# Second attention: stacked operands of chunks 1 to 3 by DMA through DRAM, chunk 0 by matmuls; full rows beside the smallest diagonal steps

## What is computed

```
b, s, _ = x.shape                      # 1, 2048; 16 heads of size D = 8, 4 kv heads
q = (x @ Wqa @ Wqb).reshape(b, s, H, D)
kv = (x @ Wkva @ Wkvb).reshape(b, s, KVH, D, 2)
k, v = (kv[..., 0], kv[..., 1])
q, k = _rope(q), _rope(k)              # rotation of pairs of features by position
k, v = repeat(k, 4), repeat(v, 4)      # each kv head serves 4 query heads
out = softmax(causal(q k^T * D ** -0.5)) v   # then @ Wout + bout, times a gate, plus x
```

## Time and profile before

| | us |
|---|---|
| median of 3 runs | 1277.96 |
| range of the runs | 1269.67 to 1278.08 |
| profiled execution, its time | 1279.31 |
| its span, first to last instruction | 1277.5 |
| from the first stack to step 0 | 454.6 to 505.9 |
| the 160 steps | 505.9 to 974 |

### The profile page before, as it was taken

One profiled execution on the slowest core, in us unless ns is written; L12 is line 12 of the kernel. 1 busy time (PEld: TensorE's weight loads), 2 busy tenths in 40 slices (PEclk: granted clock), 3 DMA queues, 4 the chain that ended last, 5 costly groups with the idle time before them and its releaser, 6 DMA issues.

```text
span 1277.5 us, 17760 instructions
## 1 busy us (share of the span) xinstructions
PE 1161.5 (91%) x6079; PEld 624.4 (49%) x6079; DVE 927.9 (73%) x1803; ACT 761.2 (60%) x1120; POOL 174.8 (14%) x142
## 2 busy tenths in 40 slices
PE   3888668999999788999999999999997799999998
PEld 2333344577777423333233222322223688888886
DVE  5699986355555746688896879898933788888885
ACT  1635436588788322456555756566776666666664
POOL 0000010498899400000000000000000000000000
PEclk9898777799999865899997989998999799999999
DMA  5000010789985300000000000000000211111001
GB/s 166 1 0 1 0 46 11 168 195 208 201 190 130 132 1 1 2 2 2 2 1 2 2 1 2 1 2 1 1 2 1 93 58 58 58 57 57 1 1 33
DMA packets 35660, 60.36 MB, mean 47 GB/s; under 512 B 14138, under 2 KB 27706, under 8 KB 30266
## 3 DMA queue, kind: packets, MB, share of 16 engines
q1 hardware_dynamic: 35586, 59.36, 18.4%
HBM read 57.59 MB, written 1.64 MB: 46 GB/s over the span
## 4 chain that ended last, share of the span: by engine, by line
PE 65%; DVE 24%; ACT 5%; issue 4%; POOL 1%; DMA 0%; SPq 0%; DVEq 0%; POOLq 0%; ACTq 0%
PE ps L868 10%; PE ps L1075 10%; PE ps L869 10%; PE ps L870 10%; PE ps L1004 7%; DVE arena_b L1824 6%; PE ps L1053 5%; PE ps L965 4%; DVE arena_b L1575 3%; PE ps L1017 2%; PE ps L1060 2%; DVE arena_b L1756 1%; PE ps L730 1%; POOL parts L685 1%; ACT arena_b L1388 1%
## 5 line engine op out<-in xcount | busy, mean ns | idle before, releaser
L1388 ACT ACTIVATE arena_b<-ps 128x1024 f32<-128x1024 f32 (+3 forms) x320 | 274.9, 895 | 155.0 <-PE ps L1053 133.6
L868 PE MATMUL ps<-parts 128*128 128x512 f32 x640 | 253.6, 396 | 8.7 <-POOL parts L685 6.3
L870 PE MATMUL ps<-parts 128*128 128x512 f32 x640 | 250.3, 391 | 0.0
L869 PE MATMUL ps<-parts 128*128 128x512 f32 x640 | 250.2, 391 | 0.0
L1824 DVE TENSOR_REDUCE arena_b<-ps 128x1 f32<-128x512 f32 x384 | 237.6, 682 | 16.6 <-PE ps L1004 15.2
L1004 PE MATMUL ps<-arena_a 48*128 48x128 bf16 (+3 forms) x832 | 187.2, 323 | 11.1 <-DVE arena_b L1824 3.2
L685 POOL TENSOR_TENSOR parts<-arena_b,parts 128x512 fp32r<-128x512 f32 x128 | 166.8, 1311 | 69.7 <-ACT parts L1325 65.1
L1075 PE MATMUL ps<-arena_b 128*32 128x512 f32 (+3 forms) x1280 | 160.0, 573 | 0.0
L1053 PE MATMUL ps<-arena_a 50*128 50x512 bf16 (+3 forms) x832 | 151.5, 318 | 4.9 <-issue 2.6
L1004 PEld LDWEIGHTS ps<-arena_a 48*128 48x128 bf16 x832 | 60.5, 97 | 185.6 <-DVE arena_b L1824 115.8
L1756 DVE SCALAR_TENSOR_TENSOR arena_b<-ps,arena_a 128x512 f32<-128x512 f32 x128 | 87.0, 688 | 87.5 <-PE ps L870 87.5
(11 more groups left out here) (268 smaller groups left out, 1198.4 us busy)
## 6 DMA issues: line engine op xcount, KB each, us to landing
arena_a<-root_weights SPq DMA_DIRECT2D x60, 512.0 KB, 6.4
arena_b<-expert_weights SPq DMA_DIRECT2D x7, 1024.0 KB, 5.6
wslot<-in_L_ffn_up_w SPq DMA_DIRECT2D x8, 256.0 KB, 6.7
wslot<-in_L_ffn_down_w SPq DMA_DIRECT2D x8, 256.0 KB, 7.3
wslot<-in_L_ffn_w_gate SPq DMA_DIRECT2D x8, 256.0 KB, 2.9
wslot<-in_L_ffn_w_up SPq DMA_DIRECT2D x8, 256.0 KB, 3.3
wslot<-in_L_ffn_w_down SPq DMA_DIRECT2D x8, 256.0 KB, 4.4
arena_b<-in_spread SPq DMA_DIRECT2D x1, 1152.0 KB, 6.2
```

Of the source, the lines that this page charges most:

```text
L868: mm(bank, w(0), x(0), start=start, stop=False)
L869: mm(bank, w(0), x(1), start=False, stop=False)
L870: return mm(bank, w(1), x(0), start=False, stop=stop)
L1388: a(probs[:, s % 2, 2 * pair:2 * pair + 2, off:CW], ps[:, 2 + 2 * pair:4 + 2 * pair, off:CW], ACT.Exp, scale=scale).then_inc(p2_exp, 1)
```

## The change

Only chunk 0 is still stacked by matmuls (12 stacks: 3 ahead, 9 as slots). For chunks 1 to 3 SP writes the split parts `q3` and `k3` to DRAM and loads them back to their strips, once for each product and strip. `kst` gets a second copy: `kst[.., half, ..]` holds keys only in the strip `half`, zeros elsewhere, so that a matmul over all 128 rows gives the same sum as one over the strip; POOL zeroes `kst` and chunks 1 to 3 of `qst` first. `WIDE` says which score slots use 128 rows: those ahead of and beside step 0, and those beside the step that follows a step with 256 or 128 columns left, so the last step of an item and the first of the next. `kst` copies of chunk 0 are two ScalarE instructions. SLOTS[0] now ends with item 0's maxima (16 scores, 3 stacks, 1 maxima), steps 0 and 1 have 8 slots each, and of the 576 scores 139 are wide. POOL's bias addition waits for the fourth item's maxima instead of norm(2).

```diff
 def attention_schedule():
+    stacks, needed = [], []
+    for c, g in ITEMS:
+        for x in [(0, g, 0), (0, g, 1), (0, g, 2)]:
+            if c == 0 and x not in stacks:
+                stacks.append(x)
+        needed.append(len(stacks))
...
-            if c < NC - 1 and (len(blocks) - 1 - k) < HPG - 1:
-                scores.append(("stack", -1, c + 1, n % G1, k + HPG - 1 - len(blocks)))
             if k == 0 and n > 0:
                 scores.append(("maxima", n - 1))
+            scores += [("stack", -1) + x for x in ahead[k * len(ahead) // len(blocks):(k + 1) * len(ahead) // len(blocks)]]
...
-    end = {n: max(k for k, x in enumerate(scores) if x[1] == n and x[0] != "maxima") + 1 for n in range(NITEM)}
-    slots = [scores[:end[1]]]
-    done = end[1]
+    end = {n: scores.index(("maxima", n)) + 1 for n in range(NITEM)}
+    done = end[0]
+    slots = [scores[:done]]
...
-        for n in range(2, NITEM):
+        for n in range(1, NITEM):
             if first[n] - 3 >= k:
-                want = min(end[n] + HPG + 1, len(scores)) - done
+                want = end[n] - done
                 rate = max(rate, -(-want // (first[n] - 2 - k)))
...
-        qst = take([G1, NC, 2, CW], BF16)
-        kst = take([G1, T], BF16)
+        qst = take([NC, G1, 2, CW], BF16)
+        kst = take([2, G1, T], BF16)
...
-        PRE = 3 * G1
+        PRE = NEEDED[0]
...
+        def light(s):
+
+            n, j = STEPS[s]
+            return j - TPC * ITEMS[n][0] >= 2
+
+        WIDE = [k < 2 or light(k - 2) for k, part in enumerate(SLOTS) for _ in part] + [False] * len(LAST_SLOTS)
...
+            def stack_k():
+
+                sp.wait_ge(ksplit_ready, 1)
+                for c in range(1, NC):
+                    sp.dma_start(k_dram[:, :, chunk(c)], k3[32 * c:32 * c + 32]).then_inc(st_k, 16)
+                sp.wait_ge(kzero, 1)
+                for half in range(2):
+                    r = half * STRIP + KROWS
+                    sp.dma_start(kst[r:r + 2, half, :, CW:T], A["ones"].rearrange("(a b) n -> a b n", a=1)
+                                 .broadcast_to([2, G1, T - CW])).then_inc(ld_k, 16)
+                sp.wait_ge(st_k, 16 * (NC - 1))
+                for half in range(2):
+                    for y, (_, x) in enumerate(PRODUCTS):
+                        r = half * STRIP + y * HD
+                        sp.dma_start(kst[r:r + HD, half, :, CW:T],
+                                     k_dram[:, x, CW:T].rearrange("(g e) t -> e g t", e=HD)).then_inc(ld_k, 16)
+
+            def stack_q(c):
+
+                sp.wait_ge(split_ready, c + 1)
+                sp.dma_start(q_dram[c].rearrange("h e a t -> (h e) a t"), q3[:, c]).then_inc(st_q[c], 16)
+                sp.wait_ge(qzero, 1)
+                sp.wait_ge(st_q[c], 16)
+                for half in range(2):
+                    heads = q_dram[c].rearrange("(m s) e a t -> s e m a t", s=2)[half]
+                    for y, (x, _) in enumerate(PRODUCTS):
+                        r = half * STRIP + y * HD
+                        sp.dma_start(qst[r:r + HD, c].rearrange("p g a t -> p (g a) t"), heads[:, :, x, :])\
+                          .then_inc(ld_q[c], 16)
...
+            stack_k()
+            stack_q(1)
             for n in range(NITEM):
                 maxima_rows(n)
+                if n < NC - 2:
+                    stack_q(n + 2)
...
-            pool.wait_ge(ln_xn, 3 * NC)
+            pool.wait_ge(moe_down, N_IT0 * MU)
+            pool.wait_ge(moe_prod, N_IT0 * MU)
+            g.memset(kst[:, :, :, :].rearrange("p h g t -> p (h g t)").bitcast(F32), 0.0).then_inc(kzero, 1)
+            g.memset(qst[:, 1:NC].rearrange("p c g a t -> p (c g a t)").bitcast(F32), 0.0).then_inc(qzero, 1)
+
+            pool.wait_ge(nm_ready, G1)
             pool.wait_ge(wo1_ready, 1)
             g.tensor_tensor(xt[:, :, :], xt[:, :, :], bo1[:, :].unsqueeze(1).broadcast_to([P, NT, D]), ALU.add)\
                 .then_inc(bias_ready, 1)
...
-                    c, g = n // G1, n % G1
-                    pe.wait_ge(stack_ready, 3 * (n + 1))
-                    r = slice(STRIP * (i % 2), STRIP * (i % 2) + KROWS)
+                    c, g = ITEMS[n]
+                    pe.wait_ge(stack_ready, NEEDED[n])
+                    if c > 0:
+                        pe.wait_ge(ld_k, 16 * 2 * (len(PRODUCTS) + 1))
+                        pe.wait_ge(ld_q[c], 16 * 2 * len(PRODUCTS))
+                    if m == 0:
+                        pe.wait_ge(kzero, 1)
+
+                    r = slice(0, P) if WIDE[m] else slice(STRIP * (i % 2), STRIP * (i % 2) + KROWS)
...
-                    a(kst[:, g, chunk(c)], ps[:, bank, :], ACT.Identity, bias=onerow[:, :]).then_inc(stack_ready, 1)
+                    for half in range(2):
+                        r = slice(half * STRIP, half * STRIP + STRIP)
+                        last = a(kst[r, half, g, chunk(c)], ps[r, bank, :], ACT.Identity, bias=onerow[r, :])
+                        if half == 0:
+                            step(last)
+                    last.then_inc(stack_ready, 1)
```

More of the change, by code:

```diff
@@ L47 @@
 STRIP = 64
-NITEM = NC * G1
+ITEMS = tuple((c, g) for c in range(NC) for g in range(G1))
+NITEM = len(ITEMS)
+LAST_OF = {c: n for n, (c, g) in enumerate(ITEMS)}
 E1, F1 = 8, 512
@@ L61, in attention_schedule @@
 def attention_schedule():
-    steps = [(n, j) for n in range(NITEM) for j in range(TPC * (n // G1 + 1))]
+    steps = [(n, j) for n, (c, _) in enumerate(ITEMS) for j in range(TPC * (c + 1))]
     first = {}
@@ L71, in attention_schedule @@
         first.setdefault(n, k)
+    stacks, needed = [], []
[4 more added lines that the diff above has]
+        needed.append(len(stacks))
     scores = []
[L73 to L74 removed]
+    for n, (c, _) in enumerate(ITEMS):
         blocks = [("scores", t, u) for t in range(TPC * c, TPC * c + TPC) for u in range(c)]
         blocks += [("diag", 0, 0), ("below3", 0, 0), ("below12", 0, 0)]
+        ahead = stacks[needed[n]:needed[n + 1]] if n + 1 < NITEM else []
         for k, (what, t, u) in enumerate(blocks):
             scores += [(what, n, t, u, i) for i in range(HPG)]
[L79 to L80 removed]
             if k == 0 and n > 0:
                 scores.append(("maxima", n - 1))
+            scores += [("stack", -1) + x for x in ahead[k * len(ahead) // len(blocks):(k + 1) * len(ahead) // len(blocks)]]
     scores.append(("maxima", NITEM - 1))
[L84 to L86 removed]
+    end = {n: scores.index(("maxima", n)) + 1 for n in range(NITEM)}
+    done = end[0]
+    slots = [scores[:done]]
     late = {}
[L88 to L89 removed]
+    for n, (c, _) in enumerate(ITEMS):
+        s = first[n] + TPC * (c + 1)
         late.setdefault(s + 1, []).append(("out", n))
[L91 to L93 removed]
+        if n == LAST_OF[c]:
+            late.setdefault(s + 2, []).append(("turned", c))
+            late.setdefault(s + 3, []).append(("product", c))
     for k in range(len(steps)):
         rate = 0
[L97 removed]
+        for n in range(1, NITEM):
             if first[n] - 3 >= k:
[L99 removed]
+                want = end[n] - done
                 rate = max(rate, -(-want // (first[n] - 2 - k)))
@@ L105, in attention_schedule @@
     tail = [x for k in sorted(late) for x in late[k]]
-    return steps, slots, tail
+    return steps, slots, tail, stacks, needed
 def adaln_two_layers(nc, A, out):
@@ L283, in adaln_two_layers @@
         sc_dram = nc.dram_tensor("root_weights", [E0, T], F32).ap()
+        q_dram = nc.dram_tensor("q_parts", [NC, H1, HD, NPART, CW], BF16).ap()
+        k_dram = nc.dram_tensor("k_parts", [G1 * HD, NPART, T], BF16).ap()
         cw_dram = nc.dram_tensor("expert_weights", [E1, T], F32).ap()
@@ L376, in adaln_two_layers @@
         vzero = sem("vzero")
+        qzero = sem("qzero")
+        st_k = sem("st_k")
+        st_q = [sem(f"st_q{c}") for c in range(NC)]
+        ld_k = sem("ld_k")
+        ld_q = [sem(f"ld_q{c}") for c in range(NC)]
+        kzero = sem("kzero")
         wt_tr = sem("wt_tr")
@@ L423, in adaln_two_layers @@
         out_ready = sem("out_ready")
-        STEPS, SLOTS, LAST_SLOTS = attention_schedule()
+        STEPS, SLOTS, LAST_SLOTS, STACKS, NEEDED = attention_schedule()
         NFIRST = len(SLOTS[0])
-        PRE = 3 * G1
-        STACKS = [(c, g, kind) for c in range(NC) for g in range(G1) for kind in range(3)]
+        PRE = NEEDED[0]
         def slot_bank(m):
@@ L442, in slot_before @@
             return ORDER[same[-1]] if same else None
+        assert [x[2:] for x in ORDER if x[0] == "stack"] == STACKS[PRE:]
         NITEM0 = min(k for k, x in enumerate(SLOTS[0]) if x[1] == 1 or x[0] == "maxima")
+        def light(s):
+            n, j = STEPS[s]
+            return j - TPC * ITEMS[n][0] >= 2
+        WIDE = [k < 2 or light(k - 2) for k, part in enumerate(SLOTS) for _ in part] + [False] * len(LAST_SLOTS)
         HALF = GP * NC
@@ L1030, in slot @@
                     c = what[1]
-                    pe.wait_ge(slot_read, READ["out", c * G1 + G1 - 1])
```

(6 more changed lines are left out.)

33 lines of the change are left out of this document (14 added, 19 removed).

## The result

| | before | after |
|---|---|---|
| median (range), 4 runs each | 1274.45 us (1269.67 to 1278.08) | 1231.73 us (1227.46 to 1235.01) |
| ratio to before, 95% interval | | 0.969 (0.963 to 0.975) |
| profiled execution, its span | 1279.31, 1277.5 us | 1230.85, 1229.0 us |

What follows compares the result with a forecast made beforehand. VectorE was taken to set the pace undisturbed, with PE the limit at about half clock in six windows. Prologue terms of -13.9 and loop terms of -37.6 made -51.5 us, so 1226 us, range 1206 to 1262.

Steps and rivals of the forecast that it cites:

- (1) to (3): Prologue: nine of twelve stacks go, -11.4; k stack moves into step 1, -1.4; shorter way to step 0, -5.1.
- (5): Prologue: full rows under the first scores make the clock rise earlier, -3 us, bounds 0 and -11.
- (4): Prologue: POOL's two memsets hold up VectorE's small instructions in norm(2), +7.0 us, bounds 0 and 12.6.
- (6): Loop: stacks fall from 31 to 6, 25 at 0.75 us each, -18.9, bounds -10 and -22.
- (8) and (9): Loop: full rows prevent clock falls in six windows, -22.2 us, and the low clock of the first 76.4 us, -5.
- (10): Loop: full-row scores no longer run side by side in pairs; VectorE hides most, +3 us, at most +17.7.
- (12): SP's extra stores and loads ahead of the first row of maxima: 0 us, high end +13.
- (13): Loop: fewer scores per step in items 4 to 7 change the order, not the number: no effect.
- A: Clock falls as before, because rows multiplying zeros, or rows at all, don't count: 1256 us, chance 0.15.
- B: Work left on PE becomes the bound, through exposed waits or lost pairs: 1241 to 1279 us, chance 0.09.
- C: SP's DMAs or POOL's memsets come late, at their high ends: 1245 us, chance 0.10.
- D: Without the dense stack matmuls the early loop's clock falls for good: slower than before, 1301 us, chance 0.04.

Runs made afterwards that it cites:

- e1_narrow: The changed kernel with every score matmul over 48 rows again, nothing else different: 1268.76 us, ratio 0.993 to before.
- e4_pieces: The changed kernel with POOL's two memsets cut into 56 pieces of 256 words each: 1235.78 us, ratio 0.971 to before.
- e7_wide_all: The changed kernel with all 576 scores over 128 rows: 1269.47 us, ratio 0.994 to before.
- e12_wide_start: The changed kernel with full rows only in the 22 scores ahead of the loop and beside step 0: 1254.92 us, ratio 0.994 to before.
- e11_wide_early: The changed kernel with full rows only in 59 scores ahead of and beside the first 17 steps: 1249.34 us, ratio 0.989 to before.
- e3_all_stacks: The changed kernel with all 48 stacks made by matmuls and no DMA through DRAM: 1265.64 us, ratio 1.001 to before.
- e10_stacks_narrow: e3_all_stacks with no full rows anywhere, so 48-row scores and the short start: 1285.89 us, ratio 1.018 to before.
- e9_rows_first: The changed kernel with memsets in pieces, load waits once per chunk, item 15 full-row, rows of maxima issued before q's loads: 1229.23 us.
- e6_one_wait: The changed kernel with waits for stack loads once per chunk instead of at 528 score slots: 1237.19 us, ratio 0.977 to before.

## Why the prediction was right, and where it was not

The touched stretch was to lose 51.5 us and lost 45.4; the median was to be 1226 and is 1232. By its own steps:

- **(1) to (3)**, fewer stacks ahead, k stack moved, short way to step 0: -17.9 expected. Stack to first score brought -11.1 (for -11.4), the k stack -1.3 (24.5 against 23.2 in e1_narrow, for -1.4), transposition to step 0 -5.4 (for -5.1). Step 0 came at 485.1 us, from experts that ended 7.1 us earlier, so 492.2 for the 491 foreseen. Right, though the k stack's share is within the scatter told under (5).
- **(4)**, the memsets: +7.0 expected, +6.1 measured, through two instructions of 0.17 us stretched to 3.50 and 3.80, each to a memset's end. e4_pieces, which takes only that away, won 6.0. Shown. The Trainium skill, "SBUF — State Buffer", "Who interferes with whom", has tensor_scalar among the instructions that can take the port pair which VectorE shares with POOL, and whoever holds that pair blocks the other for a whole instruction; the trace agrees, in that just these instructions wait until the memset's end, though no row shows how they used the ports. It is the rule that fits here, not the one I had weighed.
- **(5)**, the clock in the start: -3 expected. First score to transposition is 22.3 us with full rows and 23.2 without (e1_narrow), but three kernels with the code of the kernel after in this stretch took 20.1 (e7_wide_all), 22.3 (e12_wide_start) and 23.8 us (e11_wide_early). A gain of 1 is within that scatter; 3 was too large. At step 0 nothing was left of it: from the first stack it comes 31.5 us later in the kernel after and 31.4 in e1_narrow.
- **(6)**, 25 stacks: -18.9 expected at 0.75 each. No single run isolates it in the old order. In the new one, e3_all_stacks against after, a stack costs 38.8 / 36 = 1.08. Taking the measured -32.8, less the falls at the price below and 4.5 for scores, leaves -16.2, or 0.65 each. This is a remainder, and so holds whatever else was mis-sized. The 1.08 has two ScalarE copies for each k stack in it. So 0.65 to 1.08, with 0.75 inside.
- **(8) and (9)**, the clock in the loop: -27.2 expected. The mechanism was right in what it foresaw, every fall but item 15's is gone, and comes back without full rows. The size was the term that failed: I priced a fall at length x (1 - clock), as if PE alone set the pace, which makes 0.5 us per low us. The runs give 0.31 to 0.36 early and 0.40 to 0.42 later, most likely since part of the time VectorE or ScalarE would have set the pace anyway (VectorE is busy in 92% of steps 48 to 127 once the falls are gone). With 8.8 low us fewer in steps 0 to 15 and 44.4 later: 2.9 + 18.2 = -21.1. These 6 us are as large as the whole miss; the smaller terms, +2 in (5) and about +3 in (6) against -1 in (4), -3 in (10) and -1 in (11), cancel.
- **(10)**, full rows: +3 expected, within 1 by the line through two kernels where VectorE covers them; the high bound is real without cover (e7_wide_all, 32.9 us).
- **(11)**, waits: +1 expected, 0 measured. My count was wrong too: 528 x 2 are new, but the wait for the stacks drops from 573 to 46, so 529 were added.
- **(12)**, SP's DMAs: 0 expected. In the kernel after about 1 us (4.2 against 3.1), up to 7 in other kernels. I looked at the time of issues; what counts is landings behind one another.
- **(13)**, order: 0 expected. Without full rows it is not neutral: with the short start most later falls are gone in the one trace of e10_stacks_narrow and more of the low clock lies in the loop. Full rows covered both, so that it came out near nothing was luck.

**The rivals.** A (falls stay) is refuted: from step 4 on, the only fall left in the loop is where no full row stands. B is refuted for the waits and bounded for the rows. C was real in both its halves, 6 us of POOL, already in the sum, and 1 us of SP. D (stacks gone, so the early clock falls) I gave 0.04, and it is the one I misread. Its mechanism exists: e1_narrow is low for 66.8 us of its first 80. It did not decide because full rows stand in just these steps, and my argument against it, the stretch from 872 us, spoke of steps with plenty of other work. Without them the change would have been worth nothing in the loop (468.3 against 468.6 us) and little in all: ratio 0.993, with 1.001 as the end of its interval.

The closeness of 1226 and 1232 says less than it seems: terms (8) and (9) were 6 us too large, (5) 2, while the interaction of the two halves, some 12 us in the loop, was not in the sum as such. That the sum still came near is in part luck.

## What to carry to other kernels

Before dense matmuls are taken off TensorE, ask what keeps its clock up afterwards: here that alone turned a gain of 33 us in the loop into nothing, and widening 139 score matmuls to all 128 rows, where VectorE set the pace, brought it back for almost no time. Price a low clock by what bounds the stretch, not by half of its length. A row on which everything waits should be issued ahead of bulk transfers of the same queue, and large memsets beside a latency-bound chain of VectorE should be cut into pieces.

## What the runs showed of the hardware

- PE's busy share does not tell whether its clock holds. Steps 0 to 15 of e1_narrow: PE 96% busy, clock 0.58; of the kernel after: 93% busy, 0.96. The difference is 48 or 128 rows, the others zero, and with 128 the scores run one after the other and not in pairs; no run parts the two. In e12_wide_start PE was busy for all of 27.30 us with the clock at 0.50. By the Trainium skill, "TensorE: Matmul & The Clock Gate", Part 1, the clock follows how busy PE is; with busy taken as a matmul in flight, the trace differs.
- Some VectorE instructions beside a POOL memset wait until it ends, though it only writes: a TENSOR_SCALAR of 128x4 went from 0.17 us to 3.50 and 3.80, each to a memset's end. Others don't: the statistics of norm(2), four of them beside the first memset, took their usual 0.87 us. In pieces of 256 words (0.27 to 0.30 us each) the same TENSOR_SCALAR took 0.17 to 0.36 us.
- The landing of a 4 KB row depends on what was issued ahead of it: issued 20 us behind the last load, step 0 started 2.5 us later (e9_rows_first, 483.09 to 485.54); issued right behind 12 loads of q, 7.3 us (e6_one_wait, 489.17 to 496.45) or 4.9 (e7_wide_all); issued 5.4 us behind them, again 2.5 (e1_narrow).
- A wait of 51 ns on PE's queue, 528 of them twice, took no time at all in a loop with PE 96% busy (e6_one_wait against the kernel after, stretches within 0.4 us).
